# Cross attention with 16 dims per head: scores of two heads at once on halves of 64 rows, turns a step later, one bank for projections

## The reference

```python
q = split(q_in, qw, qb) * hd ** (-0.5)        # 8 x 16 heads x 112 x 16
k = split(k_in, kw, kb)                       # 8 x 16 heads x 375 x 16
v = split(v_in, vw, vb)
s = jnp.einsum('bhqd,bhkd->bhqk', q, k)
a = jax.nn.softmax(s, axis=-1)
o = jnp.einsum('bhqk,bhkd->bhqd', a, v)
return o.transpose(0, 2, 1, 3).reshape(B, Sq, C) @ pw + pb
```

## Time and profile before

| | us |
|---|---|
| median of 3 runs | 2165.87 (2164.4 to 2177.83) |
| profiled execution, its own time | 2163.83 |
| its span, first to last instruction | 2162.0 |
| updates of X in L0_ca (L1501) | 183.50, 210.89, 238.68, 266.07, 293.61 and so on |
| updates of X in L1_ca (L1501) | 858.65, 886.08, 913.60, and the last two 1022.62, 1042.70 |

### The profile page before, as it was taken

The page is one execution under the profiler, slowest core; times in us unless marked ns, Lnnn a source line. Parts: engine busy times, 40 slices in busy tenths (PEclk is TensorE's granted clock), DMA queues, the critical chain, the costliest instruction groups (busy, mean ns, idle before and its releaser), DMA issues.

```text
span 2162.0 us, 34309 instructions
## 1 busy us (share of the span) xinstructions
PE 1812.8 (84%) x10658; PEld 1289.2 (60%) x10658; DVE 1326.3 (61%) x3343; ACT 866.9 (40%) x2497; POOL 641.2 (30%) x710
## 2 busy tenths in 40 slices
PE   5969998389938689999869999695886969999888
PEld 4747775278837576776755554483443835555457
DVE  5856666111148765666757667595776956656555
ACT  4635554022216425555324444242331434545421
POOL 2325554200032334555500000040000415455433
PEclk9979998599969889999979999797998979999979
DMA  4000000378830000010100010101001000001100
GB/s 165 29 21 16 15 0 1 117 248 301 284 131 1 0 0 23 15 46 0 64 9 13 15 65 0 49 1 59 0 0 53 18 0 12 21 10 29 50 1 17
DMA packets 34247, 102.76 MB, mean 48 GB/s; under 512 B 2624, under 2 KB 25696, under 8 KB 26976
## 3 DMA queue, kind: packets, MB, share of 16 engines
q1 hardware_dynamic: 32608, 97.79, 13.1%
q0 software_dynamic: 1536, 3.67, 0.5%
HBM read 93.20 MB, written 8.26 MB: 47 GB/s over the span
## 4 chain that ended last, share of the span: by engine, by line
PE 55%; issue 15%; DVE 13%; POOL 8%; ACT 4%; DMA 3%; SPq 0%; POOLq 0%; DVEq 0%; ACTq 0%
PE ps L909 8%; PE ps L792 7%; POOL arena L1786 6%; PE ps L732 4%; PE ps L944 4%; PE ps L805 4%; PE ps L737 3%; PE ps L855 3%; PE ps L787 3%; PE ps L837 3%; PE ps L1039 2%; PE ps L1023 2%; DMA arena<-rows_hbm 2%; PE ps L832 2%; PE ps L724 2%
## 5 line engine op out<-in xcount | busy, mean ns | idle before, releaser
L1786 POOL TENSOR_TENSOR arena<-arena,rinv 112x375 f32<-112x375 f32 (+1 forms) x448 | 371.4, 829 | 524.5 <-DVE rinv L1460 513.6
L805 PEld LDWEIGHTS ps<-cst,arena 112*125 112x125 f32 (+1 forms) x1408 | 206.1, 182 | 182.5 <-POOL arena L1786 81.2
L792 PE MATMUL ps<-arena 128*112 128x112 f32 (+1 forms) x1024 | 277.3, 385 | 14.6 <-ACT arena L1148 13.0
L805 PE MATMUL ps<-cst,arena 112*125 112x112 f32 (+1 forms) x1408 | 237.7, 281 | 57.0 <-POOL arena L1786 56.7
L1148 ACT ACTIVATE arena<-ps,negmax 112x375 f32<-112x375 f32 (+1 forms) x384 | 190.5, 501 | 188.1 <-DVE negmax L1455 187.2
L1455 DVE TENSOR_REDUCE negmax<-ps 112x1 f32<-112x375 f32 (+1 forms) x288 | 159.4, 553 | 157.9 <-PE ps L792 157.6
L1834 POOL TENSOR_TENSOR w_split_sb<-wml,w_split_sb 128x512 fp32r<-128x512 f32 (+1 forms) x40 | 44.9, 1124 | 572.4 <-ACT w_split_sb L1197 570.5
L1469 DVE COPY arena<-ps 125x336 f32<-125x336 f32 x384 | 189.7, 494 | 12.0 <-PE ps L805 11.2
L909 PE MATMUL ps<-h_split_sb,w_split_sb 128*128 128x448 f32 x768 | 179.7, 384 | 8.4 <-DVE h_split_sb L1583 4.3
L1148 ACT ACTIVATE arena<-arena,negmax 112x112 f32<-112x112 f32 (+1 forms) x256 | 125.4, 491 | 140.6 <-DVE negmax L1444 109.0
L732 PE MATMUL ps<-wat,arena 128*125 128x256 f32 (+1 forms) x704 | 177.3, 390 | 2.5 <-ACT arena L1095 1.8
(11 more groups left out here) (202 smaller groups left out, 3063.1 us busy)
## 6 DMA issues: line engine op xcount, KB each, us to landing
wml<-in_wm_L_moe SPq DMA_DIRECT2D x21, 1028.0 KB, 5.8
wml<-in_wm_L_moe SPq DMA_DIRECT2D x21, 1024.0 KB, 6.3
craw<-in_ctx SPq DMA_DIRECT2D x40, 375.0 KB
wml<-in_wm_L_m SPq DMA_DIRECT2D x3, 3072.0 KB, 13.2
wat<-in_wa_L_ca SPq DMA_DIRECT2D x2, 2560.0 KB, 9.2
wml<-in_wm_L_m SPq DMA_DIRECT2D x2, 2048.0 KB, 9.5
rows_hbm<-wml SPq DMA_DIRECT2D x2, 1344.0 KB, 13.9
arena<-rows_hbm SPq DMA_DIRECT2D x21, 128.0 KB, 5.4
```

Of the source, the lines that this page charges most:

```text
L792: last = mm(ps[0:S, blk.bank_at(s), i * blk.nk:(i + 1) * blk.nk], qz[:, parity(b), head_of(u) if blk.dh == 16 else u], kT[:, parity(b), u ...
L805: last = nc.tensor.transpose(ps[0:blk.kp, T_BANK + s % blk.t_banks, o:o + S], buf[:, i * blk.nk + q * blk.kp:i * blk.nk + (q + 1) * blk.kp ...
L1786: pool.tensor_tensor(p3, p3, r3, ALU.mult).then_inc(scaled, 1)
```

## The change

L0_ca and L1_ca get the same schedule and join `PAIRS`. Scores of two heads go out together at even steps, each on 64 partitions, into four score banks (0 to 3) in place of two. For that `spread_q` writes copies for 4 heads in place of 8, with a new mask `mask16of64`. `lag` grows from 3 to 4, and the probabilities get eight buffers in place of four. Banks 2 and 3 are gone for the pieces, so all of them use bank 7, and the output projection moves to the second half of bank 6, behind the weighed values; the first weighing of a batch now waits for the update too. The pieces lie on even steps but for V1.

```diff
     "L0_ca": dict(
-        plan={2: ["XT"], 4: ["CT0"], 8: ["CT1"], 10: ["Q"], 12: ["K0"], 13: ["K1"], 14: ["V0"], 15: ["V1"]},
+        plan={2: ["XT"], 4: ["CT0"], 6: ["CT1"], 8: ["Q"], 10: ["K0"], 12: ["K1"], 14: ["V0"], 15: ["V1"]},
         dve={0: ["norm"], 2: ["cnorm"]},
-        pool={12: ["spread0"], 14: ["spread1"]},
-        out_step=6, lag=3, s_banks=2, t_banks=2, w_banks=[7, 3, 2], out_bank=7),
+        pool={11: ["spread0"], 13: ["spread1"]},
+        out_step=6, lag=4, s_banks=4, t_banks=2, w_banks=[7], out_bank=6),
...
     "L1_ca": dict(
-        plan={3: ["XT"], 5: ["CT0"], 6: ["CT1"], 9: ["Q"], 12: ["K0"], 13: ["K1"], 14: ["V0"], 15: ["V1"]},
+        plan={2: ["XT"], 4: ["CT0"], 6: ["CT1"], 8: ["Q"], 10: ["K0"], 12: ["K1"], 14: ["V0"], 15: ["V1"]},
         dve={0: ["norm"]},
-        pool={11: ["spread1"], 13: ["spread0"]},
-        out_step=6, lag=3, s_banks=2, t_banks=2, w_banks=[7, 3, 2], out_bank=7),
+        pool={11: ["spread0"], 13: ["spread1"]},
+        out_step=6, lag=4, s_banks=4, t_banks=2, w_banks=[7], out_bank=6),
...
-PAIRS = ("L3_ca",)
+PAIRS = ("L0_ca", "L1_ca", "L3_ca",)
...
-        self.nprobs = 4
+        self.nprobs = 8 if self.pairs and dh == 16 else 4
+        self.out_at = D if self.out_bank == 6 else 0
...
+            if blk.pairs:
+                ins.tensor_tensor(qz[:, parity(m), 4 * c:4 * c + 4], qs[:, c].unsqueeze(1).broadcast_to([P, 4, S]),
+                                  cs("mask16of64", 4).unsqueeze(2).broadcast_to([P, 4, S]), ALU.mult).then_inc(spread, 1)
+                return
...
                     if g == blk.wg - 1:
                         wait(pe, o_done, count(st["o"], blk.no, b))
+                        if blk.out_bank == O_BANK:
+                            wait(pe, out_done, count(st["out"], 1, b))
...
-                        last = mm(ps[0:S, blk.out_bank, 0:D], oT[:, c], wo[:, c], start=c == 0, stop=c == blk.cq - 1)
+                        last = mm(ps[0:S, blk.out_bank, blk.out_at:blk.out_at + D], oT[:, c], wo[:, c], start=c == 0, stop=c == blk.cq - 1)
```

More of the change, by code:

```diff
@@ L243, in columns @@
     put("mask16", 8)
+    put("mask16of64", 4)
     put("mask64", 2)
@@ L311, in build @@
         pT = view["pT"].rearrange("p (t k h s) -> p t k h s", t=4, k=KC, h=HG)
-        probs = view["probs"].rearrange("p (t k) -> p t k", t=6)
+        at_probs = list(sizes).index("probs")
+        at_probs = sum(list(sizes.values())[:at_probs])
+        probs = arena[:, at_probs:at_probs + 8 * 448].rearrange("p (t k) -> p t k", t=8)
         ms = view["ms"].rearrange("p (t k) -> p t k", t=2)
@@ L1498, in update @@
                     dve.wait_ge(out_full, count(st["out"], 1, b, 1))
-                    W = ps[0:S, blk.out_bank, 0:D]
+                    W = ps[0:S, blk.out_bank, blk.out_at:blk.out_at + D]
                     if blk.out_bias is not None:
@@ L1899 @@
     put("mask16", (rows16 // 16 == np.arange(8)[None]).astype(np.float32) * np.float32(0.25))
+    put("mask16of64", (rows16 // 16 % 4 == np.arange(4)[None]).astype(np.float32) * np.float32(0.25))
     put("mask64", (rows16 // 64 == np.arange(2)[None]).astype(np.float32) * np.float32(0.125))
```

## The result

The changed kernel takes 2177.23 us (2170.76 to 2187.21, 17 runs) against 2170.94 us before (2159.64 to 2177.83, 17 runs): a ratio of 1.0041, with a 95% interval of 1.0027 to 1.0056. That is 6 us more than before, where 15 us less were forecast (2151 us), and above the range, 2119 to 2174. The profiled execution took 2173.39 us (span 2171.6), against 2163.83 (span 2162.0).

What follows compares the result with a forecast made beforehand. TensorE was taken to set the pace of both blocks, with VectorE right behind. Full batches -21, last batches -2, batch 0 -3 and block starts +12 gave -14 us, about 2151 us; range 2119 to 2174 for 8 in 10.

Steps and rivals of the forecast that it cites:

- +6 us a block, 12 in all: Start of L0_ca and L1_ca: pieces sharing one bank wait for evacuations, 7 us less 1 us for the clock.
- 1.0 us, seven times: Block starts: every piece but the first waits for an evacuation, 0.27 until ScalarE starts, 0.57, and 0.15 until TensorE resumes.
- less 1 us since the clock comes up in the midst of them anyway: Block starts: 1 us taken off the 7 us of piece waits, as the clock was expected to rise during the pieces.
- 11 us if the thinner work keeps the clock at 0.50 to the first score: Block starts: upper bound of the added cost, against +6 us expected and 4 us as lower bound.
- a rival with 0.11: Block starts: clock stays at half through both, waits half a microsecond longer each, 2158 to 2172 us; chance 0.11.
- the first score 15 us behind the first piece: Block starts: sign to look for in the profile after, the distance from first piece to first score.
- gives 1 us in each block: Eighth batch of L0_ca and L1_ca: no pieces, bound by VectorE's 0.95 us a step; gains 1 us each, 2 in all.
- the clock falls inside the batches: Rival: a batch at half clock costs some 19 us more; two such batches make it 2189 us; chance 0.08.
- L1_ca 25.4, L0_ca 26.6: Forecast us per full batch: 23.6 of TensorE work plus added waits, gains of 2.1 and 0.9 a batch.
- The three waits: Each full batch: weighing behind the update 0.9 us, V1 behind V0 0.7, late weighing 0.2 in L1_ca, 1.4 in L0_ca.
- those two rivals: Clock falling inside the batches, chance 0.08; pair matmuls running one behind the other, some 2215 us, chance 0.04.
- the cover holds: Rival: the three waits vanish in unseen slack, a batch takes 23.6 us, 2118 us in all; range 2115 to 2140, chance 0.27.

Runs made afterwards that it cites:

- The spread banks: Changed kernel with batch 0's eight pieces in L0_ca and L1_ca sent to eight different banks: 2154.49 us, ratio 0.9925 to the kernel before.
- the waits added before: Kernel before the change, with each batch 0 piece in L0_ca and L1_ca also waiting for the evacuation of the piece ahead: 2191.58 us, ratio 1.0101.
- the filler: Changed kernel plus one unused 256-column matmul ahead of each batch 0 piece but the first in L0_ca and L1_ca: 2166.84 us, ratio 0.9988.
- the run with the earlier projection: Changed kernel with out_step 5 in place of 6 in L0_ca and L1_ca, so projection and update stand one step earlier: 2175.22 us, ratio 1.003.

## Why the prediction was wrong

It was wrong in the sum, 2151 against 2177 us, and in the sign. By its own steps, against the profiled executions (-14 forecast, +9.6 measured):

- **"+6 us a block, 12 in all" is the step that failed.** It measured +10.7 and +11.7, 22.3 in all. The eight pieces behind one bank were seen, and the round trip of "1.0 us, seven times" was of the right kind: with the clock up early it measured some 5.2 us a block. Wrong was "less 1 us since the clock comes up in the midst of them anyway". I took the clock of the old start for that of a start which the change makes thinner. The text had the right case as its bound, "11 us if the thinner work keeps the clock at 0.50 to the first score", and as a rival with 0.11, whose 2158 to 2172 us the measurement still passes, for the reasons below. The spread banks, the waits added before and the filler showed it: starts of 10.6 and 8.6, 21.0 and 19.7, 14.8 and 14.2 us. The sign given for it, "the first score 15 us behind the first piece", failed with 20.1 and 20.7.
- **The last batch "gives 1 us in each block"** was wrong as well: it cost 0.4 and 5.1 us in the two profiled executions. The wait "behind the update" was worked out for a middle batch. In the last batch the statistics stand behind the update too, and copy 3 behind those, so 0.9 becomes 3.9 us, and TensorE is then at half clock for 10.3 us. Moving the statistics removed both. How long the half clock lasts was luck: in two other kernels with this wait it was 6.8 us, and the loss in L1_ca would have been 2.5. This is also a part of the rival "the clock falls inside the batches", which the prediction put at 0.08 and at some 19 us.
- **"L1_ca 25.4, L0_ca 26.6"** measured 26.05 and 26.9; the mechanism was right and three sizes were off. Two steps cost 0.82 + 0.41 + 0.41 = 1.64 us, not 1.56, since the turn ahead of a pair is as slow as the one behind it: 8 x 0.08 = 0.6 us a batch. The waits of the scores that four banks take away came to 0.9 us, not 1.2: in the batch behind the update at 913.60 the turns at 932.58 and 933.85 take 0.55 and 0.84 in place of 0.32, and the scores behind them 0.72 in place of 0.63. And V1 ahead of a pair costs 0.1 more. The waits that the change adds came out 0.3 us below the forecast in L1_ca, 1.5 against 1.8, and 0.7 below in L0_ca, 2.3 against 3.0. Together that is the difference, to within 0.1 us.
- **The three waits were right in place and sign, and near in size**: "0.9 us" behind the update measured 0.88 in L1_ca and 0.69 in L0_ca, V1's "0.7 us" some 0.6, the late weighing's "1.4 us" in L0_ca 1.03; the "0.2 us" in L1_ca did not show (the weighing at 922.77 follows its turn, at 922.26, by 0.51 us).
- The middle with batch 0 gave -17 us of the forecast -24. The clock fell in no middle batch (1.00 from the first to the sixth update of L1_ca, 874.4 to 1004.8), and a pair takes 0.82 us where two scores took 1.26, so those two rivals are out, and "the cover holds" too, since the waits are there.

The gap of 24 us is thus 10 at the starts, 7.5 in the last batches and 7 in the middle, less 1 in the rest of the program. Left open is that last 1 us: behind the last update of L1_ca, where the kernels here differ in nothing but where the statistics stand, the profiled executions take 1115 to 1124 us. Left open too is what makes the clock stay down for 3, 7 or 10 us behind the wait in the last batch.

## What to carry to other kernels

A buffer saved in the steady loop is paid for where the loop isn't: walk through the first and the last round with the new buffers and the new order, since one bank that costs 0.6 us a batch in the middle cost 11 us at each start. When a change thins TensorE's work in a stretch that begins at half clock, price that stretch at half clock to its end, or keep the engine busy through it. When a consumer moves a step later, look in every round, the last above all, at what else stands ahead of its producer on that producer's engine.

## What the hardware showed that I had not expected

- The price of a 64-row pair lies on both sides of it: the turn ahead and the turn behind take 0.41 us in place of 0.32, and a projection ahead of a pair 1.05 in place of 0.87 (in the run with the earlier projection).
- A start with TensorE busy 18.96 of 24.00 us stayed at a granted clock of 0.50 for all of it. With one matmul of 256 columns in each gap it was at 1.00 some 3.5 us behind the first piece.
- One wait of 3.88 us, in work that had run at 1.00, was followed by 10.3 us at 0.51 although TensorE was busy in all of them, and by as much in the run with the extra matmuls. The same wait was followed by 6.8 us at 0.50 in two other kernels. A wait of 2.95 us at the same place in the kernel before left the clock at 1.00, and with the same rows there but waits at the starts it was followed by 3.4 us at 0.50. In the last batch of L0_ca the clock fell in both kernels, for 3.5 us before and for 6.8 us after.
